# Earlier rounding steps for the gated products of a two-layer transformer kernel

## The reference, cut to what matters

```
def fp4_quant_dequant(x):                      # blocks of 16 along the last dim
    scale = max(max(abs(block)) / 6, 1e-12)
    q = nearest of (0, 0.5, 1, 1.5, 2, 3, 4, 6) to abs(x / scale), with x's sign, * scale
h = silu(fp4_linear(x, w_gate)) * fp4_linear(x, w_up)      # 512 x 352
return fp4_linear(h, w_down)                               # rounds h first
```

## Time and profile before

| what | value |
|---|---|
| median of 3 runs | 2107.48 us (2105.41 to 2107.88) |
| profiled execution: its time, its span | 2107.8 us, 2105.3 us |
| mean granted clock of TensorE | 0.980 of full speed |
| busy share PE, DVE, ACT, POOL | 92%, 73%, 65%, 53% |
| one frame in the middle | 124.80 us |

### The profile page before, as it was taken

How to read it: one execution, slowest core, us unless ns; L and a number is a source line. 1 busy time by engine, 2 the same in 40 slices (tenths; PEclk the granted TensorE clock), 3 DMA queues, 4 the chain that set the end, 5 groups by cost and what they waited for, 6 DMA issues and landing times.

```text
span 2105.3 us, 49557 instructions
## 1 busy us (share of the span) xinstructions
PE 1934.3 (92%) x17353; PEld 1264.0 (60%) x17353; DVE 1540.2 (73%) x5223; ACT 1366.8 (65%) x3733; POOL 1125.6 (53%) x1671
## 2 busy tenths in 40 slices
PE   3789999999999999999999999999999999998978
PEld 1455665756566575656657566665656657565645
DVE  7558778687776868778686877868777686876646
ACT  1777585676857667585766858577685766758531
POOL 4675374645637465473746547374563746545220
PEclk9779999999999999999999999999999999999989
DMA  5102021110301112030210202121020111101010
GB/s 146 27 9 44 4 39 23 39 24 9 53 4 38 24 24 38 4 59 3 39 24 18 44 4 44 18 39 24 12 49 4 38 24 20 37 4 34 4 32 6
DMA packets 172651, 59.36 MB, mean 28 GB/s; under 512 B 139643, under 2 KB 169971, under 8 KB 172403
## 3 DMA queue, kind: packets, MB, share of 16 engines
q1 hardware_dynamic: 172403, 56.19, 13.8%
HBM read 14.22 MB, written 4.19 MB: 9 GB/s over the span
## 4 chain that ended last, share of the span: by engine, by line
PE 59%; DVE 14%; ACT 13%; issue 7%; POOL 6%; DMA 0%; SPq 0%; DVEq 0%; ACTq 0%; POOLq 0%
PE ps L1127 11%; PE ps L1198 8%; PE ps L1263 8%; PE ps L1208 7%; PE ps L1141 5%; ACT ring L949 5%; PE ps L1117 4%; DVE ring L583 3%; PE ps L1248 3%; ACT pb L958 3%; PE ps L1186 2%; DVE lin L615 2%; PE ps L1106 2%; PE ps L1174 2%; POOL ring L848 2%
## 5 line engine op out<-in xcount | busy, mean ns | idle before, releaser
L848 POOL TENSOR_SCALAR ring<-ring,row_rcp,tau_row 128x128 f32<-128x128 f32 (+3 forms) x1024 | 626.5, 620 | 681.4 <-DVE row_rcp L590 681.4
L949 ACT ACTIVATE ring<-ring,neg_max 128x128 f32<-128x128 f32 (+3 forms) x1024 | 570.7, 558 | 514.7 <-DVE neg_max L583 504.6
L1127 PE MATMUL ps<-identf,ring 128*128 128x128 f32 x2560 | 380.1, 287 | 5.9 <-POOL ring L848 4.0
L958 ACT ACTIVATE pb<-ps 128x512 f32<-128x512 f32 x640 | 348.4, 583 | 25.2 <-PE ps L1127 21.1
L583 DVE CUSTOM_DVE_ANT_1 ring<-ps,bias_t 128x384 f32<-128x384 f32 (+1 forms) x496 | 286.7, 614 | 54.3 <-PE ps L1117 47.0
L1127 PEld LDWEIGHTS ps<-identf,ring 128*128 128x128 f32 x2560 | 279.0, 143 | 78.6 <-issue 42.7
L1263 PEld LDWEIGHTS ps<-ed_t,h 128*128 128x128 f32 (+1 forms) x1920 | 254.6, 191 | 97.2 <-issue 93.7
L1263 PE MATMUL ps<-ed_t,h 128*128 128x128 f32 (+1 forms) x1920 | 270.6, 277 | 0.0
L1208 PE MATMUL ps<-xn1T,eu_t 128*128 128x512 f32 (+1 forms) x480 | 256.5, 616 | 1.4 <-DVE h L639 1.3
L1198 PE MATMUL ps<-xn1T,eg_t 128*128 128x512 f32 (+1 forms) x480 | 254.8, 612 | 3.1 <-DVE h L632 2.8
L1117 PE MATMUL ps<-qkT 32*128 32x128 f16 (+3 forms) x1024 | 201.5, 308 | 47.2 <-DVE neg_max L583 28.2
(11 more groups left out here) (150 smaller groups left out, 2771.8 us busy)
## 6 DMA issues: line engine op xcount, KB each, us to landing
x_t<-x SPq DMA_DIRECT2D x16, 256.0 KB, 2.8
x<-x SPq DMA_DIRECT2D x16, 256.0 KB, 2.9
o_rows<-o_stack SPq DMA_DIRECT2D x256, 16.0 KB
out<-x SPq DMA_DIRECT2D x16, 256.0 KB, 2.3
qkT<-qkx SPq DMA_TRANSPOSE x128, 3.2
bias_t<-bias SPq DMA_DIRECT2D x1, 1536.0 KB, 7.8
eg_t<-eg SPq DMA_DIRECT2D x1, 860.0 KB
eu_t<-eu SPq DMA_DIRECT2D x1, 860.0 KB
```

Source lines behind the costliest of these rows:

```text
L848: pool.tensor_scalar(e, e, row_rcp[:, m % 2, r:r + 1], tau_row[:, i, HG * g + r:HG * g + r + 1], ALU.mult, ALU.add).then_inc(p_ok.sem, 1)
L949: act.activation(e, e, ACT.Exp, bias=neg_max[:, n % 2, r:r + 1], scale=-1.0, accum_out=row_sum[:, n % 2, r:r + 1]).then_inc(exp_ok.sem, 1)
L958: act.activation(pb[:, c % NPB, :], bank(turn_bank(q)), ACT.Relu).then_inc(t_taken[q % 2].sem, 1)
L1127: last = pe.transpose(o[:, r * P:(r + 1) * P], ring_of(i, r)[:, k * P:(k + 1) * P], idf)
```

## The change

The tables of slots for the rounding of `hid` are gathered into one dictionary, read through `hidden_at(b)`. The gates, maxima, step, divisions and turns stay where they were. Three groups move, for every sequence: the constants (DVE) from slots 48, 50, 52, 54 to 42, 43, 44, 45; additions and subtractions (POOL) from 56/57, 58/59, 60/61, 62/63 to 44/45, 46/47, 48/49, 50/51; the last multiplications (POOL) from 64, 66, 68, 70 (slots 0, 2, 4, 6 of the next frame) to 52, 54, 56, 58. Nothing is added or removed.

```diff
-GATE0 = (11, 13, 16, 18)
-HID_AMAX, HID_STEP, HID_SCALED = (18, 19, 34, 35), 36, (38, 39, 40, 41)
-HID_MAGIC, HID_ADD, HID_SUB, HID_MUL = (48, 50, 52, 54), (56, 58, 60, 62), (57, 59, 61, 63), (64, 66, 68, 70)
-TURN_H, FUTURE_V, FUTURE_Y = (ATT + 11, ATT + 13, ATT + 13, ATT + 15), ATT + 61, ATT + 63
+HIDDEN = (
+    dict(gate=(11, 13, 16, 18), amax=(18, 19, 34, 35), step=36, scaled=(38, 39, 40, 41), magic=(42, 43, 44, 45),
+         add=(44, 46, 48, 50), sub=(45, 47, 49, 51), mul=(52, 54, 56, 58), turn=(ATT + 11, ATT + 13, ATT + 13, ATT + 15)),
+)
+FUTURE_V, FUTURE_Y = ATT + 61, ATT + 63
...
+def hidden_at(b):
+
+    return HIDDEN[min(b, len(HIDDEN) - 1)]
...
-                if p in HID_MAGIC:
-                    hidden_magic(b, HID_MAGIC.index(p))
+                if p in hidden_at(b)["magic"]:
+                    hidden_magic(b, hidden_at(b)["magic"].index(p))
...
-                if p in HID_ADD:
-                    t = HID_ADD.index(p)
+                if p in hidden_at(b)["add"]:
+                    t = hidden_at(b)["add"].index(p)
...
-                if f == -1 and s == GATE0[0]:
+                if f == -1 and s == QKV0 + T:
```

More of the change, by code:

```diff
@@ L76 @@
 PACK_O = tuple(ATT + NS * (g + 1) + 9 for g in range(G))
-TURNS = (("x", (TURN_X,)), ("xq", (TURN_XQ,)), ("hid", TURN_H), ("xn1", (TURN_X1,)),
+TURNS = (("x", (TURN_X,)), ("xq", (TURN_XQ,)), ("xn1", (TURN_X1,)),
          ("q32", (TURN_Q32,)), ("intra", INTRA), ("o1", (TURN_O1,)))
 EXTRAS = (("fx", (FUTURE_X,)), ("fv", (FUTURE_V,)), ("fy", (FUTURE_Y,)), ("kv", KV), ("lin", LIN), ("tot", TOT))
+def hidden_at(b):
+    return HIDDEN[min(b, len(HIDDEN) - 1)]
 def at(table, p):
@@ L122, in __init__ @@
                     self.score[name, b, k] = len(self.score)
-                for name, k in at(TURNS, p):
+                for name, k in at(TURNS + (("hid", hidden_at(b)["turn"]),), p):
                     if name != "intra" or p % 2:
@@ L128, in __init__ @@
                         gate_ticket(("qkv", layer, b, p - p0), (p - p0) % 2)
-                for layer, places in enumerate((GATE0, GATE1)):
+                for layer, places in enumerate((hidden_at(b)["gate"], GATE1)):
                     if p in places:
@@ L773, in beside @@
                     fp4_magic(x_m[:, :], xq[:, :], x_magic, b)
-                if p in HID_AMAX:
-                    hidden_amax(b, HID_AMAX.index(p))
-                if p == HID_STEP:
+                if p in hidden_at(b)["amax"]:
+                    hidden_amax(b, hidden_at(b)["amax"].index(p))
+                if p == hidden_at(b)["step"]:
                     hidden_step(b)
-                if p in HID_MAGIC:
-                    hidden_magic(b, HID_MAGIC.index(p))
+                if p in hidden_at(b)["magic"]:
+                    hidden_magic(b, hidden_at(b)["magic"].index(p))
                 if p == ROUTER - 3:
@@ L874, in beside @@
                     stack_low(b, 0, p - QKV0 - 4)
-                if p in HID_SCALED:
-                    t = HID_SCALED.index(p)
+                if p in hidden_at(b)["scaled"]:
+                    t = hidden_at(b)["scaled"].index(p)
                     pool.wait_ge(h_step_ok.sem, h_step_ok.at(b, 2))
                     times_block(part(hid, t), part(hid, t), q_step[:, 0, t * NT:(t + 1) * NT], NT, h_scaled)
-                if p in HID_ADD:
-                    t = HID_ADD.index(p)
+                if p in hidden_at(b)["add"]:
+                    t = hidden_at(b)["add"].index(p)
                     pool.wait_ge(h_magic.sem, h_magic.at(b, 2 * t + 2))
                     pool.tensor_tensor(part(hid, t), part(hid, t), part(q_m, t), ALU.add).then_inc(h_added.sem, 1)
-                if p in HID_SUB:
-                    t = HID_SUB.index(p)
+                if p in hidden_at(b)["sub"]:
+                    t = hidden_at(b)["sub"].index(p)
                     pool.wait_ge(h_added.sem, h_added.at(b, t + 1))
                     pool.tensor_tensor(part(hid, t), part(hid, t), part(q_m, t), ALU.subtract).then_inc(h_rounded.sem, 1)
-                if p in HID_MUL:
-                    t = HID_MUL.index(p)
+                if p in hidden_at(b)["mul"]:
+                    t = hidden_at(b)["mul"].index(p)
                     pool.wait_ge(h_rounded.sem, h_rounded.at(b, t + 1))
@@ L994, in beside @@
                     stack_high(b, 0, p - QKV0 - 3)
-                for layer, places in enumerate((GATE0, GATE1)):
+                for layer, places in enumerate((hidden_at(b)["gate"], GATE1)):
                     if p in places:
                         tanh_gate(layer, b, places.index(p))
-                for name, t in at((("hid", TURN_H),), p):
+                for name, t in at((("hid", hidden_at(b)["turn"]),), p):
                     turned(("hid", b, t), hqT[:, t, :, :].rearrange("p c n -> p (c n)"), 3 * P)
```

## The result

The changed kernel takes 2130.46 us (median; 2128.82 to 2132.24), the kernel before 2107.68 us on the same chip: ratio 1.0109, 95% interval 1.0096 to 1.0122, 22.8 us slower. The prediction was 2124 us, range 2106 to 2149. The one profile of the variant "all slots old" was taken at a mean granted clock of 0.65 (2657 us); its slots are not read, and its time in the table is the median of its nine other runs.

The account below looks back on a forecast made before the run. PE was taken to set the pace in slots 43 to 48, ACT's norm and POOL's addition at the frame's start. 14 x 1.1 = 15.4, less 1.6, plus 2.4 gave 16.2 us: about 2124 us, range 2106 to 2149.

Parts of the forecast that it names:

- DVE against POOL, slots 42 to 45: Slots 42 to 45: four moved pairs of constants delay DVE, making PE 1.1 us late per frame, for 14 frames.
- first pair: Slot 42: these two constants fall into DVE's 1.51 us wait ahead of `lin`, with POOL idle; cost nothing.
- second: Slot 43: pair of constants whose second half waits for POOL's scaling, making the next bias 0.9 us late.
- third: Slot 44: pair of constants whose halves both wait for POOL, making the `lin` pair 0.8 us late.
- the term per frame: Frames 1 to 14: PE 1.1 us late in each, against 0.11 us gained at the frame's start.
- DVE catches up: From slot 48: DVE recovers because its old 1.66 us pair has gone, while PE carries its 1.1 us on.
- longer cascade: Rival, slots 42 to 48: late maxima delay ACT, then line 632; constants meet POOL twice each; 2135 to 2149; chance 0.18.
- The frame's start: Slot 3: DVE's line 478 loses an overlapping POOL multiplication, gaining 0.11 us x 15 frames = 1.6 us.
- faster: Rival, frame's start: the chain comes through `rstd`, so a 0.79 us multiplication comes off each frame; about 2100; chance 0.13.
- Around frame 0: Ahead of frame 0: multiplications now ahead of `rstd` make DVE late, +2.4 us; within frame 0, nothing within 2 us.
- The term for the rest of frame 0: Frame 0 itself: additions leave slot 60 but enter slots 44 to 51 at the same density; nothing, within 2 us.

Follow-up runs that it names:

- all slots old: The changed kernel's code with all slots of the old table, a control: 2108.10 us, ratio 0.9998 to the kernel before.
- constants only: The changed kernel with additions, subtractions and multiplications back at their old slots, constants still at 42 to 45: 2110.84 us, ratio 1.0016 to the kernel before.
- additions from 46: The changed kernel with POOL's additions, subtractions and multiplications two slots later: 2118.72 us, ratio 1.0047 to the kernel before.

## Why the prediction was right, point by point

**DVE against POOL, slots 42 to 45.** The steps came in as written: first pair free; second 0.31 and 0.70 (0.9 us late forecast, 0.8 measured); third 1.5 us (1.2 forecast); `lin` 0.8 us late (0.8); bias of slot 46 1.8 us late (1.7); PE 1.2 us late at its product of slot 48 (1.1). The reading that a constant waits for the running POOL instruction was taken from one pair of the old trace; the variants "constants only" and "additions from 46" showed it. The Trainium skill, page "SBUF — State Buffer", section "SBUF: two separate sides", calls this an exclusive lock for a whole instruction; by that rule, the traces agree, with constants of 0.33 and 0.80 us and POOL instructions that grow by about 0.1 us. The page names as the condition a two-port mode or two inputs in SBUF. The constants have one input; the strided form waited too, and no run here shows which mode either form ran in.

**What was mis-sized: the term per frame.** It was 1.1 less 0.11, so 1.0 us; measured are 1.34 in the example frame and 1.37 on the mean of frames 2 to 14. The prediction followed PE's delay to slot 48 and had it carried on unchanged, with "DVE catches up". ACT doesn't at once: its exponentials of slots 46 and 47 come late, its copy `nd` behind them ends at 1120.94, and PE's second turn in slot 48 needs the bank that this copy frees. The trace of the change, line 1133 in these slots:

```profile
L1133 PE MATMUL ps<-identf,ring x8: 272/273/328, 1120.3 to 1121.4; 128*128 128x128 f32 x8
...
  ACT nd L923: 0.3, 1
```

That is 0.25 us more per frame: the product of line 1214 begins 1.17 us behind line 1133 where it was 0.92. This is the rival "longer cascade" in a small form. The sum of 1.19 and 0.25 less 0.11 is 1.33, which is what the windows of the example frame give (126.14 against 124.80). The other 0.04 of the mean is the two values of slots 32 to 34, of which the prediction had nothing and whose cause is not known.

**The frame's start.** The gain of 0.11 us per frame was right in size and place. Line 478, now 484, at its minimum throughout:

```profile
L484 DVE TENSOR_SCALAR x_step<-x_step x16: 180/181/182, 11.8 to 1792.4; 128x32 f32<-128x32 f32 x16
```

The rival "faster" needed `rstd` on the chain: ACT's norm stands where it stood, 4.5 us behind slot 0 (1033.13 less 1028.61, as 1019.39 less 1014.87 before), so 10.7 us less POOL work around the frame's turn bought 0.1 us.

**Around frame 0.** `rstd` came 2.8 us later; 0.6 of that is a later start of the whole frame, which varies as much among the variants, and 2.2 stand against the 2.4 forecast. DVE's wait for it grew from 2.84 to 5.07 us, by 2.2:

```profile
55.35 3.01 POOL L830 TENSOR_TENSOR hid<-hid,q_step 128x352 f32<-128x352 f32 x4
58.32 0.20 POOL L834 TENSOR_TENSOR rstd<-moments,eps_t 128x4 f32<-128x4 f32 x1
...
59.65 0.16 DVE L548 SCALAR_TENSOR_TENSOR shift<-moments,rstd 128x4 f32<-128x4 f32 x1 [5.07 <-POOL rstd L836]
```

Slot 2 of frame 0 grew by 1.64 us of the 2.4 forecast. The term for the rest of frame 0, taken as nothing within 2 us, was 2.2 us, just outside that: its slots 42 to 56 grew by 3.8, slots 60 to 62 shrank by 1.2.

**The sum.** Between the two profiled executions frames 2 to 14 grew by 13 x 1.37 = 17.9 us, frame 1 by 1.0 and frame 0 by 3.85: 22.7 us. Frame 0 began 0.6 us later, and what follows the start of the last frame took 1.6 us less (215.4 against 217.0 us, with a granted clock of 0.90 instead of 0.86 in a stretch of 50 us); it takes 214 to 218 us in the variants too. So the spans differ by 21.7 us, and the medians by 22.8. The forecast had 14 x 0.99 = 13.8 and 2.4, 16.2 in all. Of what it lacks, 5 us are the term per frame and 1.4 us frame 0.

## What to carry to other kernels

Before an instruction is moved to a slot where its engine has time, look at what its neighbours do there: the same constant took 0.34 us beside an idle GpSimd and up to 0.9 beside a busy one, and two engines with much idle time on the average were brought together in the one place where TensorE had none. Price a move by the chain it lands in, instruction by instruction, and follow the lateness past the engine that catches up to every buffer that it frees late. Relief of an engine that is not on the chain is worth next to nothing, however full it looks: three POOL microseconds taken from the frame's start gave 0.1.

## What was not expected of the hardware

VectorE's constants over a stride of 16 elements (0.46 us instead of 0.34) wait for GpSimd's running instruction just as the dense ones do. The block maxima over the same data (0.51 us) do not. The meeting is not free for GpSimd either: the instruction that it begins while a constant still runs grows, an addition of 0.93 us to 1.01 beside the dense constants and 1.15 beside the strided ones, a scaling of 0.66 us to 0.75 and 0.88.
